# Cross attention: the projection is written to the second bank of the turned scores instead of the shared bank

## What is computed

```python
q = (x @ Wq).reshape(B, N, HEADS, hd).transpose(0, 2, 1, 3)
k = (context @ Wk).reshape(B, M, HEADS, hd).transpose(0, 2, 1, 3)
v = (context @ Wv).reshape(B, M, HEADS, hd).transpose(0, 2, 1, 3)
scores = jnp.einsum('bhid,bhjd->bhij', q, k) * scale
attn = jax.nn.softmax(scores, axis=-1)
out = jnp.einsum('bhij,bhjd->bhid', attn, v)
out = out.transpose(0, 2, 1, 3).reshape(B, N, DIM)
return out @ Wo
...
x = _layernorm(x + _L0_xattn_ref(x, ctx_768, ...), axis=-1)
```

## Time and profile before

| | us |
|---|---|
| median of 3 runs | 1436.6 |
| the profiled execution | 1436.18 |
| its span in the trace | 1434.0 |
| cross attention, first to last matmul of its loop with maxima (step 0 to 63) | 169.4 to 486.9 |
| granted TensorE clock over the span, mean | 0.97 |
| PE busy over the span | 1300.5 (91%) |

### The profile page before, as it was taken

One profiled execution on the slowest core, in us unless ns is written; L12 is line 12 of the kernel. 1 busy time (PEld: TensorE's weight loads), 2 busy tenths in 40 slices (PEclk: granted clock), 3 DMA queues, 4 the chain that ended last, 5 costly groups with the idle time before them and its releaser, 6 DMA issues. The chain is left out here.

```text
span 1434.0 us, 31566 instructions
## 1 busy us (share of the span) xinstructions
PE 1300.5 (91%) x11006; PEld 1061.7 (74%) x11006; DVE 1130.0 (79%) x2382; ACT 896.7 (63%) x1670; POOL 1165.4 (81%) x1034
## 2 busy tenths in 40 slices
PE   4766589999999769999999999988999999999998
PEld 3555467766677547777777777757999999999997
DVE  4899456666666658888888888877999999999996
ACT  2677456666666547777677676745666666666664
POOL 6344467787877649999999999986999999999997
PEclk8899599999999979999999999999999999999999
DMA  5110243434334051222212212212232232322221
GB/s 163 38 38 21 75 139 114 127 102 124 109 116 125 21 170 75 81 78 78 81 74 82 81 74 81 75 65 75 74 93 86 81 93 74 100 80 88 86 82 30
DMA packets 77182, 123.60 MB, mean 86 GB/s; under 512 B 8353, under 2 KB 45794, under 8 KB 77026
## 3 DMA queue, kind: packets, MB, share of 16 engines
q1 hardware_dynamic: 75426, 117.16, 25.7%
q0 software_dynamic: 1088, 4.19, 1.0%
q10 hardware_dynamic: 512, 0.23, 0.1%
HBM read 70.28 MB, written 51.27 MB: 85 GB/s over the span
## 5 line engine op out<-in xcount | busy, mean ns | idle before, releaser
L986 POOL TENSOR_TENSOR gather_d<-gather_e,gather_rinv 128x1024 f32<-128x1024 f32 x128 | 244.9, 1913 | 44.9 <-DVE gather_rinv L965 44.9
L1245 POOL TENSOR_TENSOR mix_c<-mix_e,mix_rinv 128x1024 f32<-128x1024 f32 x128 | 240.9, 1902 | 18.3 <-DVE mix_rinv L1233 15.2
L1313 PEld LDWEIGHTS last_Y<-kept_phi,last_cT 128*128 128x128 f32 x2048 | 248.4, 192 | 7.1
L1313 PE MATMUL last_Y<-kept_phi,last_cT 128*128 128x128 f32 x2048 | 249.1, 275 | 0.0
L814 POOL TENSOR_TENSOR cross_kd<-first_pack,kept_consts 128x624 fp32r<-128x624 f32 x128 | 155.6, 1236 | 68.3 <-DMA first_pack<-first_halves 56.8
L1329 ACT COPY last_cT<-last_T 128x1024 f32<-128x1024 f32 x128 | 128.4, 1003 | 128.7 <-PE last_T L1320 128.7
L722 DVE TENSOR_REDUCE cross_mx<-cross_S 128x8 fp32r<-128x624 f32 x128 | 103.6, 809 | 122.2 <-PE cross_S L560 122.2
L1230 DVE TENSOR_REDUCE mix_sums<-mix_e 128x16 f32<-128x1024 f32 x128 | 155.7, 1216 | 33.7 <-ACT mix_e L1204 33.2
L961 DVE TENSOR_REDUCE gather_rsum<-gather_e 128x32 f32<-128x1024 f32 x128 | 156.1, 1220 | 26.3 <-ACT gather_e L934 26.3
L980 POOL TENSOR_TENSOR gather_dl<-gather_d,gather_dh 128x512 fp32r<-128x512 f32 x128 | 166.2, 1299 | 0.0
L923 ACT COPY gather_keep<-gather_L 128x256 f32<-128x256 f32 x256 | 94.7, 370 | 104.0 <-PE gather_L L897 95.9
(11 more groups left out here) (202 smaller groups left out, 3016.3 us busy)
## 6 DMA issues: line engine op xcount, KB each, us to landing
kept_logits<-gather_keep SPq DMA_DIRECT2D x128, 256.0 KB, 2.0
mix_read<-kept_logits SPq DMA_DIRECT2D x64, 512.0 KB, 3.7
first_halves<-first_qk SPq DMA_DIRECT2D x32, 412.0 KB, 3.0
first_pack<-first_halves SPq DMA_DIRECT2D x64, 128.0 KB
first_pack<-first_halves SPq DMA_DIRECT2D x32, 206.0 KB
first_pack<-first_halves SPq DMA_DIRECT2D x64, 78.0 KB
attn_xTg<-in_xT SPq DMA_DIRECT2D x16, 256.0 KB, 2.6
kept_xres<-in_x POOLq DMA_DIRECT2D x4, 1024.0 KB, 12.2
```

The source lines that it names most:

```text
L986: pool.tensor_tensor(dd[u % 4][:].rearrange("p i (n s) -> p i n s", n=16), e[u % 2][:], rinv[u % 2][:].rearrange("p (i n) -> p i n", i=2). ...
L1245: pool.tensor_tensor(self.cc[u % 2][:], self.e[u % 2][:], self.rinv[u % 2][:].unsqueeze(2).to_broadcast([128, 16, EXPERTS]), ALU.mult)\
L1313: ins = pe.matmul(psY[t % 2][:, 0:128], cT[u % 2][:, c, :], w.yk[:, 8 * (u % 2) + c, :], start=(u % 2 == 0 and c == 0), stop=(u % 2 == 1 a ...
```

## The change

`project(n)` writes to bank 1 of `banks` for n < B - 3 = 61, and to the shared bank for the last three batches. For the former it waits for `e_low` (the exponentials of banks 0 and 1 of step n+2's scores, taken in step n+3) in place of the shared bank's last reader, and leaves `held` alone. `turned_scores(n)` gets a wait for `y_done` of `add_residual(n-3)`. `add_residual` reads the new place.

```diff
+        def projection(n):
+            return banks[:, 1, 0, :] if n < B - 3 else psM[:, 0:128]
+
         def x2_turned(n):
             return banks[:, 0, 0, :] if n < SHARED else psM[:, 0:128]
...
             def project(n):
                 pe.wait_ge(oT_ready, n + 1)
-                take_bank(y_done, n + 1)
-                pe.matmul(psM[:, 0:128], oT[n % 2][:], w.xo[:], start=True, stop=True).then_inc(pj_made, 1)
+                if n < B - 3:
+                    pe.wait_ge(e_low, n + 3)
+                else:
+                    take_bank(y_done, n + 1)
+                pe.matmul(projection(n), oT[n % 2][:], w.xo[:], start=True, stop=True).then_inc(pj_made, 1)
...
             def turned_scores(n):
                 r, b = n // 2, n % 2
                 reach(pe, e_ready, n)
+                reach(pe, y_done, n - 2)
                 reach(pe, xl_ready, n - 4)
...
             def add_residual(n):
                 dve.wait_ge(pj_made, n + 1)
                 reach(dve, x2_kept, n - 1)
-                dve.tensor_tensor(y[n % 2][:], psM[:, 0:128], w.xres[:, tokens(n)], ALU.add).then_inc(y_done, 1)
+                dve.tensor_tensor(y[n % 2][:], projection(n), w.xres[:, tokens(n)], ALU.add).then_inc(y_done, 1)
```

## The result

The changed kernel takes **1429.2 us** (median of 4 runs, 1426.35 to 1430.49) against 1436.1 us before (1435.54 to 1436.62): 7 us less, a ratio of 0.9948 with a 95% interval of [0.9932, 0.9964]. The direction was forecast; the size was not: I had predicted 3.6 us less, in a range that ended at 1431.0 (my starting point was the median of three runs, 1436.6). Its profiled execution took 1429.12 us, with a span of 1427.0.

The account below looks back on a forecast made before the run. PE bounds steady cross attention, idling before the turned maxima; 57 steps of 0.06 us plus 0.2 us in step 6 give 3.6 us less, 1433.0 us for the median, range 1431.0 to 1436.7.

Parts of the forecast that it names:

- What bounds the kernel: Steady cross attention: PE bounds it, at work 230.68 of 252 us; 17.9 us idle stand before the turned maxima.
- the two delays of a release: PE's waits: one held by a matmul itself costs 0.05 us, one on the instruction ahead 0.114 us.
- Points 1 to 3: Turned maxima load 0.26 us earlier, but turned scores, adding a free residual-sum wait, gain only 0.055, held by x2's low part.
- Point 4: The shift follows the turned scores by 0.43 us; freeing it from the copied maxima adds up to 0.01 us per step, half counted.
- Points 5 and 6: The projection's lost wait, 0.20 us in even steps, is worth nothing; SP, POOL and DMA effects are covered.
- The sum: Steps 7 to 63 give 57 times 0.06 us, 3.4 us; with step 6's 0.2 us, 3.6 us together.
- I count nothing: Steps 3 to 5: their gain runs into step 6's 1.40 us wait for SP's late store, so zero is counted.
- nothing is left: Rival: the 0.055 us margin vanishes, the shift is otherwise held, or start or low clock takes it back; 1434 to 1437, 29%.
- Its price for a step behind the stall: Step 7, behind the DMA stall at 1.2 GHz, took 6.22 us against 5.11: one such step costs 1.1 us.
- the whole wait goes: Rival: the low part is not in the way, so each step gains 0.26 us, 15 us in all; 1421.7, 5%.
- A further semaphore costs its own time: Rival: two late semaphores on the turned scores' wait each cost 0.07 us or more; 1437.4 to 1441.4, 8%.
- The signs of being wrong: Turned scores 0.26 us behind maxima, or 0.17 or more behind the low part, or pair 0.12 shorter without time gained.

Follow-up runs that it names:

- the copy in halves: Changed kernel with ScalarE's copy of the turned maxima split into two successive halves: 1424.9 us, ratio 0.9917; the same split in the kernel before: 1441.5 us.
- the old wait kept: Changed kernel with the projection again also waiting for the shared bank's last reader, as before the change: 1429.5 us, ratio 0.9945.

## Why the prediction was wrong

*What bounds the kernel, and the two delays of a release:* right. The maxima load 0.06 us behind the peak (0.05 taken), the turned scores 0.11 to 0.12 behind the low part (0.114 taken).

*Points 1 to 3:* right. The maxima start 0.26 us earlier, the low part is late next, and the idle time moves one group on. The turned scores load 0.059 us earlier behind the peak, in the mean of steps 10 to 57, where 0.055 was worked out.

*Point 4 is the step that failed.* "The shift follows 16 loads later, at 0.43 us ... this wait may have held the shift by a hundredth." I saw the copy end 0.05 us before the shift, which is exactly what a release costs by my own measure, and read it as a coincidence of two equal times. The 16 loads take 0.27, so the copy held the shift's load back by 0.155. The prediction's term for this is half a hundredth per step; the measured one is 0.12.

It is 0.12 and not 0.155 because the load behind the shift (L611, L604 before) has two chains ahead of it as well:

```profile
399.64 0.14 PEld L604 LDWEIGHTS cross_O<-kept_consts,cross_on 128*128 128x128 f32 x1
```

Before the change it stands 0.426 behind the shift's load and 0.851 behind that of the turned scores, in the mean of steps 10 to 57. In the changed kernel it stands 0.732 behind the turned scores whether the shift loads 0.271 behind them or, with the copy in halves, 0.287. So it comes 0.426 behind the shift or 0.732 behind the turned scores, whichever is later: 0.851 before, 0.732 after, a gain of 0.119. With the 0.059 of the turned scores themselves that is the whole 0.178 per step. What makes up the 0.732 isn't shown; where the next scores stand ahead of the turned ones it is 0.704.

*Points 5 and 6:* right (the old wait kept: 4.773 us per step; no new wait on POOL's keys, and POOL's wait for the DMA fell from 1.75 to 1.50 us per pair as the pair got shorter).

*The sum:* the steps gained 10 us where I had 3.4. "I count nothing" for steps 3 to 5 held, since the stall took them back. I had step 6 down for 0.2 us less, but its turned scores load 0.35 us later than before (203.87 against 203.52), because the store landed later. With that, the clock behind it and the mixing stage, the first pair of profiles gives back 3 of the 10 us, which is why the gain is missed by 3.3 us (6.9 against 3.6) and not by 6.4: by luck, the forecast looks nearer than its working was. The rival "nothing is left" named that mechanism, but for a gain of 3 us. Its price for a step behind the stall, 1.1 us, came from holding the step from 6 to 7 against one from an odd to an even step (5.11); those from even to odd take 4.85, so the price was 1.4.

*Rivals:* "the whole wait goes" (15 us) did not happen from step 5 on; the low part is in the way, but only by 0.08 us per step, the 0.26 of the steps without it less the 0.178 of those with it. "A further semaphore costs its own time" is refuted by the changed kernel's rows, where the turned scores load 0.11 to 0.12 behind the low part with both semaphores on the wait.

*The signs of being wrong* did not help: none of the three named came up, and none of them looked at the shift. What did differ was the pair of steps, 0.36 us shorter where 0.12 was forecast.

## What to carry to other kernels

Where an instruction starts just one release delay behind another engine's end, in step after step, suspect that it is held by that end, however well some other duration seems to explain the start, and test it: lengthen the one or the other. A single match can mislead the other way too, as the low part of queries and keys did in the last kernel. PE's busy share doesn't show such a gap; its weight loads do. And before pricing a wait that is taken away, walk every chain from that point to where they meet again: here there were two, one over ScalarE's copy and one over the turned scores, and the gain was set by the longer of them before and the other after.

A few repeated matmuls in a stretch tell whether it is on the path, with the result unchanged.

## What the runs showed of the hardware

A wait held by the matmul itself let its load start 0.05 us after the end of the releasing instruction of ScalarE or VectorE; a wait on an instruction of its own ahead of it, 0.11 to 0.12, whether one or two late semaphores were on it. Four matmuls of 32 rows and 128 columns on four row groups took 0.068 to 0.070 us together (16 in 0.271; eight more cost 0.139 per step). In the changed kernel a load of the full array stood 0.73 us behind the first of 32 such matmuls, and 0.43 behind the first of the last 16 where those were held up. How long PE stays at 1.2 GHz behind the same idle stretch differs between kernels that do the same work from there on, and was worth 1.7 us in one place here: more than many changes bring.
